# Thirty-two scatters of routing weights issued in a row, with one wait behind them

## The reference

```python
x = _layernorm(x + _L0_attn_ref(x, ...))
x = _layernorm(x + _L0_xattn_ref(x, ctx_512, ...))
x = _layernorm(x + _L0_ffn_ref(x, ...))
x = _layernorm(x + _L1_attn_ref(x, ...))
x = _layernorm(x + _L1_xattn_ref(x, ctx_512, ...))
x = _layernorm(x + _L1_ffn_ref(x, ...))
```

```python
scores = softmax(x @ gate_weight.T)                # T x 8
topk_w, topk_idx = top_k(scores, 2)
combine = zeros((T, E)).at[arange(T)[:, None], topk_idx].add(topk_w)
gu = einsum('th,efh->tef', x, gate_up_weights)
act = silu(gu[..., :F]) * gu[..., F:]
y = einsum('tef,te,ehf->th', act, combine, down_weights)
sgu = x @ shared_gate_up.T
y = y + (silu(sgu[:, :Fs]) * sgu[:, Fs:]) @ shared_down.T
```

## Time and profile before

| | us |
|---|---|
| median of 3 runs | 2107.75 |
| lowest and highest | 2102.79, 2109.4 |
| profiled execution: its own time | 2106.78 |
| profiled execution: span from the first to the last instruction | 2104.9 |
| PE busy | 1932.6 (92%) |
| DVE busy | 1044.6 (50%) |
| ACT busy | 711.8 (34%) |
| POOL busy | 386.6 (18%) |

### The profile page before, as it was taken

One profiled execution on the slowest core, in us unless ns is written; L12 is line 12 of the kernel. 1 busy time (PEld: TensorE's weight loads), 2 busy tenths in 40 slices (PEclk: granted clock), 3 DMA queues, 4 the chain that ended last, 5 costly groups with the idle time before them and its releaser, 6 DMA issues. The chain is left out here.

```text
span 2104.9 us, 32789 instructions
## 1 busy us (share of the span) xinstructions
PE 1932.6 (92%) x12124; PEld 1575.4 (75%) x12124; DVE 1044.6 (50%) x1836; ACT 711.8 (34%) x2275; POOL 386.6 (18%) x339
## 2 busy tenths in 40 slices
PE   8999888999999979999899999899979996999991
PEld 6777677788888757877678877677758874899990
DVE  5676753455555455333455556676755232222224
ACT  4555634344444422212221112444632211233332
POOL 2110100000000056000021100000104222644335
PEclk9999999999999989999999999999999998999995
DMA  7211051000000021000290001000015100644257
GB/s 236 59 42 42 1 193 47 1 1 1 1 1 1 1 106 60 0 0 0 92 388 6 1 31 41 1 1 1 2 46 185 66 0 0 240 136 154 80 112 204
DMA packets 73376, 135.89 MB, mean 65 GB/s; under 512 B 13457, under 2 KB 31761, under 8 KB 71185
## 3 DMA queue, kind: packets, MB, share of 16 engines
q1 hardware_dynamic: 47376, 96.28, 13.2%
q0 software_dynamic: 7888, 27.94, 4.5%
q10 hardware_dynamic: 17968, 9.71, 1.8%
HBM read 90.62 MB, written 43.29 MB: 64 GB/s over the span
## 5 line engine op out<-in xcount | busy, mean ns | idle before, releaser
L1470 PE MATMUL banks<-ternary_xth,ternary_wq 128*128 (+1 forms) x352 | 141.0, 401 | 5.3 <-DVE ternary_wq L1401 3.9
L1470 PE MATMUL banks<-ternary_xtl,ternary_wq 128*128 (+1 forms) x352 | 139.4, 396 | 0.0
L571 ACT ACTIVATE causal_pr<-banks,causal_nb 128x128 f32<-128x128 f32 x256 | 89.9, 381 | 52.3 <-DVE causal_nb L713 52.3
L97 PE MATMUL banks<-latent_vh,latent_cth 128*128 128x512 f32 x256 | 104.2, 407 | 3.5 <-DVE latent_ctl L1171 3.5
L97 PE MATMUL banks<-weights,expert_xgh 128*128 x312 | 104.8, 336 | 2.4 <-DVE expert_xgl L2083 2.4
L571 ACT ACTIVATE gqa_pr<-banks,gqa_nb 128x128 f32<-128x128 f32 x256 | 89.9, 382 | 45.5 <-DVE gqa_nb L713 45.5
L99 PE MATMUL banks<-weights,expert_xgl 128*128 x312 | 101.5, 325 | 0.0
L98 PE MATMUL banks<-weights,expert_xgh 128*128 x312 | 101.5, 325 | 0.0
L99 PE MATMUL banks<-latent_vh,latent_ctl 128*128 128x512 f32 x256 | 100.2, 391 | 0.0
L98 PE MATMUL banks<-latent_vl,latent_cth 128*128 128x512 f32 x256 | 100.1, 391 | 0.0
L1430 DVE TENSOR_TENSOR ternary_hf<-ternary_sg,banks 128x512 f32<-128x512 f32 x44 | 30.2, 687 | 135.5 <-issue 79.6
(11 more groups left out here) (462 smaller groups left out, 5538.4 us busy)
## 6 DMA issues: line engine op xcount, KB each, us to landing
x_slots<-decay_zeros SPq DMA_DIRECT2D x39, 256.0 KB, 4.6
y_slots<-decay_zeros SPq DMA_DIRECT2D x39, 256.0 KB, 4.9
y_slots<-expert_ys SPq DMA_DIRECT2D x39, 256.0 KB, 2.1
expert_xin<-x_slots SPq DMA_DIRECT2D x38, 256.0 KB, 2.9
weights_raw<-in_expert_experts SPq DMA_DIRECT2D x4, 2176.0 KB, 9.7
gqa_tw<-in_ternary_w ACTq DMA_DIRECT2D x4, 2112.0 KB, 10.7
ternary_raw<-in_ternary_w SPq DMA_DIRECT2D x11, 768.0 KB, 4.1
expert_raw<-in_expert_experts POOLq DMA_DIRECT2D x3, 2176.0 KB, 10.0
```

Of the source, the lines that this page charges most:

```text
L97: pe.matmul(out, wh, xh, start=first, stop=False, **kw)
L571: a = act.activation(pr[:, h, c, :], S.bank[2 * h + c // 4][:, (c % 4) * P:(c % 4 + 1) * P], ACT.Exp, bias=nb[:, h, c:c + 1], accum_out=su ...
L1470: a = pe.matmul(dst[:, :], wq[:, j, m, c * P:(c + 1) * P], x[:, c, toks], start=c == 0 and n == 0, stop=c == C - 1 and n == 1)
```

## The change

Two lines of POOL's stream in `shared_ffn_phase` go: the wait before every second scatter of the scores. The 32 scatters are the same, in the same order and at the same place, and the wait for all 32 behind them stays. No instruction of any engine is moved or added; 15 waits go. Behind the loop stands the end of POOL's stream in this phase, its DRAIN and the barrier.

```diff
@@ -1623,8 +1623,6 @@
                     pool.wait_ge(scattered, 16 * 2 * (t + 1))
             for n in range(2 * B):
                 at = bass.IndirectOffsetOnAxis(ap=S.pos[:, n:n + 1], axis=0)
-                if n and n % 2 == 0:
-                    pool.wait_ge(scored, 16 * n)
                 pool.indirect_dma_start(S.s_slots, at, S.score[:, n:n + 1], None).then_inc(scored, 16)
             pool.wait_ge(scored, 16 * 2 * B)
```

## The result

| | before | changed | ratio (95%) |
|---|---|---|---|
| median of 6 runs each, us | 2106.64 | 2117.38 | 1.0047 (1.003 to 1.0064) |
| lowest and highest | 2102.79, 2109.4 | 2114.46, 2124.06 | |
| mean granted clock | 0.969 | 0.964 | |

The forecast was 2088.5 us, between 2083 and 2097. The profiled execution of the changed kernel took 2124.06 us, the longest of its six, with a span of 2122.2 us.

A forecast was written before the change was run, and what follows sets the result against it. PE, busy 92%, was taken as the bound, with a 21.33 us stop at a barrier where POOL came last. 2106.78 - 19.0 (barrier) + 0.5 (DVE) - 0.5 (clock) = 2087.8, given as near 2088.5 us, range 2083 to 2097.

The forecast's parts named there:

- Issue: POOL's 32 score scatters in the shared phase: 39 us to issue in a row, the last at about 1690.
- Landing: Score scatters behind their issue: taken as strictly one after another, 3.4 us each, the last landed at 1759.
- the early end of the bounds: Last score scatter's landing if latency does not grow with more queued: 8.5 us after 1690, at 1699.
- Barrier: End of the shared phase: POOL through at 1764.5, DVE last at 1770.54, PE restarts at 1772.0; gain 19.0 us.
- Clock: PE's start of the expert phase: clock drops despite the shorter stop, most of 3.2 us paid again; -0.5 us.
- rival 1: PE's stop at the barrier: the clock does not fall, or falls late; 2085.5 us, chance 0.13.
- POOL against DVE: Shared phase, 1648 to 1690: unbroken issuing costs nothing itself, but may delay DVE's subtraction on PE's path; +0.5 us.
- Rival 4: Score scatters: piled-up partial writes disturb each other, each costing more than 4.2 us; 2133 us at 5.0; chance 0.04.
- the 0.90 for faster: Whole kernel: chance of a gain above 6.3 us, with 0.68 from the forecast and the rest from rivals.

The follow-up runs named there:

- row64: Changed kernel (no waits), scattering 64-byte rows of another tensor in place of the scores, into a buffer of 16 words a slot; 2087.24 us, 0.9915 of before.
- cap8: Kernel before, with the wait before every 8th score scatter instead of every 2nd; 2087.09 us, 0.9916 of before.
- spaced: Changed kernel with a 0.6 us POOL operation behind each scatter, so one comes every 2.0 us on average; 2091.07 us, 0.9919 of before.
- pitch64: Changed kernel with the same 4-byte scores scattered 64 bytes apart, with one more DVE operation; 2091.44 us, 0.993 of before.
- half: Changed kernel scattering only the first 64 of the 128 scores of each column; 2088.05 us, 0.9909 of before.
- cap4: Kernel before, with the wait before every 4th score scatter instead of every 2nd; 2087.55 us, 0.9915 of before.
- pitch32: Changed kernel with the 4-byte scores scattered 32 bytes apart; 2089.05 us, 0.9917 of before.
- turned: Changed kernel with the halves of the scores' address swapped, so neighbours in position lie 256 bytes apart, in a 32 KB buffer; 2088.16 us, 0.9925 of before.

## Why the prediction was wrong

- **Issue: right.** 39 us for 32 issues were forecast and 39.4 measured. The 4.30 us issue of the earlier trace rows did not come back, and I had allowed 3 us for it; that was luck, since DVE's subtraction came only at 1718.5, behind the held train. In row64 and cap8 it met an issue, which took 5.0 and 5.2 us.
- **Landing: mis-sized, without effect.** I took 3.4 us a scatter, the end at which they go in turn, and put the last landing at 1759, 111 us after the first issue. It was there 47.1 us after it, at 1703.1, and at most 7.7 us after the last issue. From the first packets, some 1.5 us after the first issue, that is 45.6 / 32 = 1.4 us each, hardly more than an issue: the early end of the bounds (51 us after the first issue) was right. POOL was out of the way by far.
- **Barrier: right.** POOL's DRAIN kept its 5.28 us, DVE was last, and PE's stop was 2.23 us instead of the 2.3 forecast.
- **Clock: right in kind.** It fell in spite of the short stop, as forecast against rival 1. In cap8, the stretches around and behind PE's restart at 1771.04 show it fall and return: 0.62, 0.53, then 1.00. The whole 3.2 us was paid again, where the forecast had taken 0.5 off: the expert phase took 2084.8 - 1771.04 = 313.8 us there, against 313.9 before.

```profile
1770.00:1774.00 4.00, 1.35 (x5) 0.98 (x6) 0.69 (x1) 0.60 (x1) 0.17 (x3) 0.62 0.48 154
1774.00:1778.00 4.00, 4.00 (x15) 4.00 (x16) 0.00 (x0) 0.34 (x1) 0.00 (x0) 0.53 0.91 252
1778.00:1782.00 4.00, 2.94 (x19) 2.44 (x18) 1.69 (x3) 1.21 (x3) 0.00 (x0) 1.00 1.03 440
```

- **"POOL against DVE": the step that failed.** It said that "the pace itself costs nothing", because PE was busy 47.79 of 48 us beside the row scatters at the same pace, and it gave +0.5 us. The term measured +27.5. The analogy carried the pace over, and not what was written: 128 rows of 2 KB land in 2.7 us, 128 neighbouring words in 5.9. Both rows stood in the prediction. It used the 5.9 only for POOL's own time, and never asked who else might pay for it. Landing time alone is no rule either: spaced's words took 6.0 us and held nobody.
- **Rival 4** had the sign ("piled-up partial writes disturb each other") with a chance of 0.04, but its price was a later landing, and the last landing came sooner than forecast. The price was paid by PE, ACT and DVE. So no case held the mechanism, and the 0.90 for faster was too sure. Without the failed term the sum holds: the eight kernels in which the train is short, slow, halved or spread came to 2087.1 to 2091.1 us, and pitch64 to 2091.4.

**What is shown and what isn't.** Shown: 32 scatters of 128 neighbouring words, 1.27 us apart, hold DVE from about 10 us on and PE from about 14, and cost the phase some 27 us; bursts of 4 or 8, a pace of 2.0 us, half the words, or words 16 bytes apart cost nothing, each tried by itself. A late load of instructions isn't it. Left open: by what path the engines are held. The DMA engines are nearly idle meanwhile (share 0.02), so it isn't their bandwidth. That single PE instructions come in even steps, and that a Silu whose product is done starts 26 us late, would fit a signal held between engines or a held read of instructions already loaded, and even the writing of the profile's own records. No run tells these apart. Between 8 and 16 in a burst no length was tried.

The best version is the one with the wait before every 8th scatter: 2087.09 us, 0.84% below before. The other kernels without a hole have ratios of 0.9909 to 0.993, whose intervals overlap with its own; among them, row64 writes no scores and half only half of them.

## What to carry to other kernels

A wait between DMAs can be a brake that protects other engines, as it was here; before taking it out, look at what each DMA writes, and try a longer interval (here 4 or 8 in place of 2) before none at all. Scatter single words to places 16 bytes or more apart if they must come in numbers. Before you carry a cost from one DMA to another at the same pace, compare their landing times too (here 2.7 against 5.9 us): a difference is a warning, though not a proof. And look for the first engine that starts late, not only at PE's busy time: in cap8 DVE's 1.87 us show how near the limit is.

## What the runs showed of the hardware

- The landing time of a scatter of 128 words depends on whether they are neighbours: 5.9 us (median, two at a time) or 6.0 (one in 2.0 us) packed, 2.2 at 16 bytes, 2.1 at 32, 64 or 256 bytes and for rows of 64 bytes.
- Under a long train of packed ones PE's matmuls start at multiples of about 0.7 us, with the DMA share at 0.02; DVE is held 5 us before PE.
- A load of 0.02 MB in the queue "instruction" took 2.1 to 3.6 us beside packed scatters (before, half, cap4, cap8, spaced), and 0.9 us beside scatters of 64-byte rows (row64) or words 32 and 256 bytes apart (pitch32, turned).
- POOL's DRAIN behind the scatters took 5.28 us whether they were issued in pairs, by 8 or all in a row; in each case all had landed before it.
